# An inverse root moved from ScalarE to guess-and-Newton on GpSimd and VectorE, and one shared-expert product in place of two

## The reference, cut to what matters

```python
shared = dot(silu(dot(h, shared_gate_w.T)) * dot(h, shared_up_w.T), shared_down_w.T)
shared = sigmoid(dot(h, shared_expert_gate_w.T)) * shared
```

```python
normalizer = maximum(abs(C.sum(-1)), exp(-max_log_D))
Cn = C / (normalizer + EPS)
h = einsum('bhst,bhtd->bhsd', Cn, vh)
mu = h.mean(-1); var = ((h - mu) ** 2).mean(-1)
hn = (h - mu) * rsqrt(var + EPS) * ln_scale
x = x + tanh(g_xattn[1]) * hn
```

## Time and profile before

| what | value |
|---|---|
| median of 3 runs | 1719.93 us (1716.78 to 1725.45) |
| the profiled execution | 1727.18 us, of it 1725.9 us span from the first to the last instruction |
| mean granted clock of TensorE | 0.946 of full |
| busy: TensorE, VectorE, ScalarE, GpSimd | 93%, 64%, 59%, 35% of the span |
| expert stage, one full step's vector work | silu 0.60 us, gating 0.69, GpSimd 1.30, cast 0.62, low part 0.69 |
| expert stage ends, cells' loop runs, block begins | about 905, 940 to 1042, 1052 us |

### The profile page before, as it was taken

One profiled execution on the slowest core, in us unless ns is written; L12 is line 12 of the kernel. 1 busy time (PEld: TensorE's weight loads), 2 busy tenths in 40 slices (PEclk: granted clock), 3 DMA queues, 4 the chain that ended last, 5 costly groups with the idle time before them and its releaser, 6 DMA issues.

```text
span 1725.9 us, 30312 instructions
## 1 busy us (share of the span) xinstructions
PE 1598.0 (93%) x10932; PEld 1270.4 (74%) x10932; DVE 1098.8 (64%) x2114; ACT 1016.4 (59%) x2049; POOL 598.6 (35%) x492
## 2 busy tenths in 40 slices
PE   5699999799999999999995994999999999999898
PEld 3256654488888888888882553788888888888687
DVE  5788884487544455444445556776877777776555
ACT  4488888354433344333334663877887887776543
POOL 3333332134345333333330002464464454443000
PEclk8699999799999999999995886999999999999899
DMA  7556663343444333333400003345344334332210
GB/s 219 167 188 205 203 197 113 125 122 105 117 115 114 97 107 107 107 107 108 114 16 9 4 3 110 107 152 172 124 132 131 123 119 151 123 117 68 74 49 25
DMA packets 111046, 196.22 MB, mean 114 GB/s; under 512 B 16721, under 2 KB 59541, under 8 KB 108073
## 3 DMA queue, kind: packets, MB, share of 16 engines
q1 hardware_dynamic: 110898, 194.29, 37.1%
HBM read 167.64 MB, written 25.73 MB: 112 GB/s over the span
## 4 chain that ended last, share of the span: by engine, by line
PE 78%; DVE 8%; ACT 5%; issue 4%; DMA 2%; POOL 1%; SPq 1%; DVEq 0%; POOLq 0%; ACTq 0%
PE bank L67 17%; PE bank L69 17%; PE bank L68 17%; PE bank L282 4%; PE bank L320 4%; PE bank L306 3%; PE bank L1844 3%; PE bank L1812 3%; PE bank L1834 1%; POOL e_hidden L1066 1%; PE bank L1348 1%; PE bank L1347 1%; ACT b_turned L1921 1%; PE bank L1358 1%; PE bank L1367 1%
## 5 line engine op out<-in xcount | busy, mean ns | idle before, releaser
L1066 POOL TENSOR_TENSOR e_hidden<-e_gated,e_comb_wide 128x512 f32<-128x512 f32 x132 | 211.1, 1599 | 347.8 <-DVE e_gated L1031 332.1
L906 ACT CAST e_hidden_hi<-e_hidden 128x512 fp32r<-128x512 f32 x132 | 82.0, 621 | 319.4 <-POOL e_hidden L1066 319.4
L1024 DVE TENSOR_TENSOR e_hidden_lo<-e_hidden,e_hidden_hi 128x512 fp32r<-128x512 f32 x132 | 98.1, 744 | 212.1 <-ACT e_hidden_hi L906 212.1
L69 PE MATMUL bank<-e_x_hi,e_weights_lo 128*128 128x512 f32 (+1 forms) x528 | 210.1, 398 | 0.0
L67 PE MATMUL bank<-e_x_hi,e_weights_hi 128*128 128x512 f32 (+1 forms) x528 | 208.9, 396 | 0.7 <-ACT e_comb_rows L866 0.7
L68 PE MATMUL bank<-e_x_lo,e_weights_hi 128*128 128x512 f32 (+1 forms) x528 | 208.9, 396 | 0.0
L1921 ACT ACTIVATE b_turned<-bank,b_swap_bias 64x512 f32<-64x512 f32 x256 | 175.0, 683 | 32.7 <-PE bank L69 28.3
L527 DVE TENSOR_REDUCE a_negmax<-bank 128x2 f32<-128x512 f32 x256 | 164.7, 683 | 32.3 <-PE bank L282 31.5
L2073 POOL TENSOR_TENSOR b_turned<-b_turned,b_rope_q 128x512 f32<-128x512 f32 x64 | 83.4, 1303 | 237.7 <-ACT b_turned L1921 237.7
L423 ACT ACTIVATE a_exp<-bank 128x512 f32<-128x512 f32 x256 | 143.7, 596 | 18.7 <-PE bank L306 10.0
L69 PE MATMUL bank<-e_weights_hi,e_hidden_lo 128*128 128x256 f32 (+1 forms) x528 | 149.1, 282 | 0.0
(11 more groups left out here) (322 smaller groups left out, 4138.5 us busy)
## 6 DMA issues: line engine op xcount, KB each, us to landing
e_comb_wide<-e_combT SPq DMA_DIRECT2D x130, 256.0 KB, 4.1
e_raw<-in_e_weights SPq DMA_DIRECT2D x64, 384.0 KB, 4.6
b_qk_hi<-b_qk_parts SPq DMA_DIRECT2D x64, 256.0 KB, 2.7
b_qk_lo<-b_qk_parts SPq DMA_DIRECT2D x64, 256.0 KB, 3.0
a_qs<-a_q_parts SPq DMA_DIRECT2D x48, 192.0 KB
a_ks<-a_k_parts SPq DMA_DIRECT2D x48, 192.0 KB
b_qk_parts<-columns SPq DMA_DIRECT2D x32, 256.0 KB, 3.4
b_vw_hi<-b_v_parts SPq DMA_DIRECT2D x16, 512.0 KB, 4.2
```

The source lines that it names most:

```text
L69: return pe.matmul(out, w_lo, x_hi, start=False, stop=stop, skip_group_check=True)
L1024: dve.tensor_tensor(lo[0:rows, :], m.hidden[at % 2][0:rows, :], hi[0:rows, :].bitcast(F32), ALU.subtract).then_inc(s.hidden_lo)
L1066: pool.tensor_tensor(m.hidden[i][0:rows, :], m.gated[i][0:rows, :], m.comb_wide[u % E_RING][0:rows, chunk * BANK:(chunk + 1) * BANK], ALU. ...
```

## The change

**The inverse root.** ScalarE's square root (L1412) goes. VectorE's piece 1 now ends with the sum of squares; the rest of the small work goes to piece 2 (for the last group it stays at piece 1), and ends with a first guess of the inverse root: the bits of the value, read as an integer, times -0.5 plus a constant. Three Newton steps follow, four small instructions each (square, times the value, times -0.5 plus 1.5, times the guess), one more product with the normaliser, and the two wide instructions. This is `finish_cells`. GpSimd runs it for groups 0, 1 and 2, VectorE for group 3. ScalarE waits before a square for `summed` in place of `rooted`, and VectorE at piece 1 of group 2 and 3 for `done` of the group two before.

**The shared expert.** Its gate and up weights lie beside each other, and are used as one operand of 128 columns: one product per step (6 matmuls) gives gate in rows 0 to 63 and up in rows 64 to 127 of one bank. ScalarE reads rows 0 to 63 and writes the silu to rows 64 to 127; everything after that, and the down weights, uses rows 64 to 127. The bank is free for the step after next when `gated` is done, where it was `silu`.

```diff
@@ gate_and_up
-        for which in range(2):
+        for which in range(1 if shared else 2):
             if which == 0 and n >= 2:
-                pe.wait_ge(s.silu, n - 1)
+                pe.wait_ge(s.gated if is_shared(n - 2) else s.silu, n - 1)
...
             for d in range(DK):
-                at = (2 * d + which) * rows
-                last = product(pe, banks[2 * i + which][0:rows, :], [t[:, at:at + rows] for t in m.split[u % E_SPLITS]],
+                at = d * P if shared else (2 * d + which) * P
+                last = product(pe, banks[2 * i + which][:, :], [t[:, at:at + P] for t in m.split[u % E_SPLITS]],
@@ experts_act
-            act.activation(m.silu[i][0:rows, :], banks[2 * i][0:rows, :], ACT.Silu).then_inc(s.silu)
+            gate = slice(0, WIDTH) if is_shared(n) else rows
+            act.activation(m.silu[i][rows, :], banks[2 * i][gate, :], ACT.Silu).then_inc(s.silu)
@@ experts_dve
-            dve.wait_ge(s.up_sums, n + 1)
+            if not is_shared(n):
+                dve.wait_ge(s.up_sums, up_products(n))
...
-            dve.tensor_tensor(m.gated[i][0:rows, :], m.silu[i][0:rows, :], banks[2 * i + 1][0:rows, :], ALU.mult).then_inc(s.gated)
+            up = banks[2 * i] if is_shared(n) else banks[2 * i + 1]
+            dve.tensor_tensor(m.gated[i][rows, :], m.silu[i][rows, :], up[rows, :], ALU.mult).then_inc(s.gated)
@@ cells_act
-        if g >= 0 and piece == 2:
-            act.wait_ge(s.rooted, g + 1)
-            act.activation(m.factor[g % 2][:, :, :], m.factor[g % 2][:, :, :], ACT.Sqrt).then_inc(s.deviation)
...
             if g:
-                act.wait_ge(s.rooted, g)
+                act.wait_ge(s.summed, g)
@@ cells_dve
+            if g >= 2:
+                dve.wait_ge(s.done, g - 1)
...
+            dve.tensor_reduce(factor[:, :, :], m.square[:, :, :, :], AX.X, ALU.add).then_inc(s.summed)
+        if g >= 0 and piece == (2 if g < M_LAST else 1):
+            inv, factor = m.total[g % 2], m.factor[g % 2]
...
+            dve.tensor_scalar(factor[:, :, :], factor[:, :, :], 1.0 / CD, CELL_EPS, ALU.mult, ALU.add).then_inc(own.tick())
             dve.wait_ge(own.sem, own.n)
+            dve.tensor_scalar(m.root[g % 2][:, :, :].bitcast(I32), factor[:, :, :].bitcast(I32), -0.5, ROOT_GUESS, ALU.mult, ALU.add).then_inc(s.rooted)
+    dve.wait_ge(s.rooted, NCHUNK)
+    dve.wait_ge(s.weighed_cells, NCHUNK)
+    finish_cells(k, m, s, dve, own, M_LAST)
...
+def finish_cells(k, m, s, engine, own, g):
+
+    factor, root, step = (t[g % 2][:, :, :] for t in (m.factor, m.root, m.step))
+    for _ in range(ROOT_STEPS):
+        engine.tensor_tensor(step, root, root, ALU.mult).then_inc(own.tick())
+        engine.wait_ge(own.sem, own.n)
+        engine.tensor_tensor(step, step, factor, ALU.mult).then_inc(own.tick())
+        engine.wait_ge(own.sem, own.n)
+        engine.tensor_scalar(step, step, -0.5, 1.5, ALU.mult, ALU.add).then_inc(own.tick())
+        engine.wait_ge(own.sem, own.n)
+        engine.tensor_tensor(root, root, step, ALU.mult).then_inc(own.tick())
+        engine.wait_ge(own.sem, own.n)
+    engine.tensor_tensor(root, root, m.total[g % 2][:, :, :], ALU.mult).then_inc(own.tick())
+    engine.wait_ge(own.sem, own.n)
...
+    engine.tensor_tensor(cells, cells, root.unsqueeze(3).to_broadcast([P, CHUNK, CELLS, CD]), ALU.mult).then_inc(s.scaled)
+    engine.wait_ge(s.scaled, g + 1)
+    engine.tensor_tensor(resid, resid, cells, ALU.add).then_inc(s.done)
@@ cells_pool
+        if g < M_LAST:
+            pool.wait_ge(s.weighed_cells, g + 1)
+            pool.wait_ge(s.rooted, g + 1)
+            finish_cells(k, m, s, pool, own, g)
```

More of the change, by code:

```diff
@@ L630, with is_shared, up_products @@
 TURN = {turn: i + 1 for i, turn in enumerate(TURNS)}
+def is_shared(n):
+    return E_UNITS[E_STEPS[n][0]][1] == PAIRS
 def expert_rows(n):
-    return P if E_UNITS[E_STEPS[n][0]][1] < PAIRS else WIDTH
+    return slice(WIDTH, P) if is_shared(n) else slice(0, P)
+def up_products(n):
+    return sum(not is_shared(v) for v in range(n + 1))
 def route_piece(chunk, n):
@@ L714, in load_comb @@
         for i in range(2 if pair < PAIRS else 1):
[L715 removed]
+            rows = slice(i * WIDTH, (i + 1) * WIDTH) if pair < PAIRS else slice(WIDTH, P)
+            sp.dma_start(m.comb_wide[r][rows, :],
                          io["e_combT"][2 * pair + i:2 * pair + i + 1, cols].broadcast_to([WIDTH, TOKENS])).then_inc(ring["comb_loaded"][r], DMA)
@@ L779, in gate_and_up @@
         u, chunk = E_STEPS[n]
-        (half, _), i, rows = E_UNITS[u], n % 2, expert_rows(n)
+        (half, _), i, shared = E_UNITS[u], n % 2, is_shared(n)
         cols = slice(half * TOKENS + chunk * BANK, half * TOKENS + (chunk + 1) * BANK)
@@ L806, in to_out @@
             tile = chunk * (BANK // P) + t
-            last = product(pe, banks[4 + tile // 2][:, (tile % 2) * D:(tile % 2 + 1) * D], [h[0:rows, t * P:(t + 1) * P] for h in m.hidden_split[n % E_HIDDEN]],
-                           [v[0:rows, GU:] for v in m.split[u % E_SPLITS]], pair == 0 and tile % 2 == 0, pair == PAIRS)
+            last = product(pe, banks[4 + tile // 2][:, (tile % 2) * D:(tile % 2 + 1) * D], [h[rows, t * P:(t + 1) * P] for h in m.hidden_split[n % E_HIDDEN]],
+                           [v[rows, GU:] for v in m.split[u % E_SPLITS]], pair == 0 and tile % 2 == 0, pair == PAIRS)
         last.then_inc(s.out_sums)
@@ L905, in experts_act @@
                 act.wait_ge(s.out_sums, at - E_HIDDEN + 1)
-            act.copy(m.hidden_split[at % E_HIDDEN][0][0:rows, :], m.hidden[at % 2][0:rows, :]).then_inc(s.hidden_hi)
+            act.copy(m.hidden_split[at % E_HIDDEN][0][rows, :], m.hidden[at % 2][rows, :]).then_inc(s.hidden_hi)
         if n < len(E_STEPS):
@@ L1023, in experts_dve @@
             hi, lo = m.hidden_split[at % E_HIDDEN]
-            dve.tensor_tensor(lo[0:rows, :], m.hidden[at % 2][0:rows, :], hi[0:rows, :].bitcast(F32), ALU.subtract).then_inc(s.hidden_lo)
+            dve.tensor_tensor(lo[rows, :], m.hidden[at % 2][rows, :], hi[rows, :].bitcast(F32), ALU.subtract).then_inc(s.hidden_lo)
         if n < len(E_STEPS):
@@ L1091 @@
 M_LATER = 6
+M_LAST = NCHUNK - 1
+ROOT_GUESS = float(0x5f3759df)
+ROOT_STEPS = 3
 def mlstm_memory(k, stack):
     sb = tensors(k, stack, "m")
-    m = namedtuple("m", "ln_scale vaug e_token cell keys log_peak log_gate peak_parts gate_parts e_rows factor total square")
+    m = namedtuple("m", "ln_scale vaug e_token cell keys log_peak log_gate peak_parts gate_parts e_rows factor total root step square")
     return m(sb("ln_scale", [P, D]), sb("vaug", [P, NB, CELLS, CD + 1]), sb("e_token", [P, NB, CELLS]), sb("cell", [P, NB, CELLS, CD + 1]),
@@ L1100, in mlstm_memory @@
              [sb(f"factor{i}", [P, CHUNK, CELLS]) for i in range(2)], [sb(f"total{i}", [P, CHUNK, CELLS]) for i in range(2)],
+             *([sb(f"{n}{i}", [P, CHUNK, CELLS]) for i in range(2)] for n in ("root", "root_step")),
              sb("square", [P, CHUNK, CELLS, CD]))
@@ L1491, in cells_pool @@
 def cells_pool(k, m, w, s):
-    pool = k.nc.gpsimd
+    pool, own = k.nc.gpsimd, k.pool_steps
     pool.wait_ge(s.scale_ready, 1)
```

32 lines of the change are left out of this document (11 added, 21 removed).

## The result

The changed kernel takes 1713.07 us (median of 20 runs, 1708.43 to 1720.91) beside 1721.61 us (20 runs, 1713.09 to 1735.2) for the kernel before on the same chip: ratio 0.994, 95% interval 0.9922 to 0.9957. That is 10.3 us less (7.4 to 13.4), where 11.2 had been predicted. (The ratio is the recorded estimate, and differences in this document are worked out from such ratios; the two medians themselves lie 8.5 us apart.) The time itself, 4.4 us over the forecast of 1708.7, lies in its range. Two more measurements of the same kernel gave 0.9941 (0.9913 to 0.9969) and 0.9955 (0.9931 to 0.9978). The profiled execution took 1716.19 us, its span 1714.8 against 1725.9, with a mean granted clock of 0.951 against 0.946.

What follows compares the result with a forecast made beforehand. The prediction took TensorE, busy 93% of the span, as the bound. Loop 12.56 less tail 5.7 plus shared expert 4.3 gave 11.2 us, so 1719.93 - 11.2 = 1708.7 us, range 1703 to 1715.

Steps and rivals of the forecast that it cites:

- The loop: mLSTM cell loop: without ScalarE's root, its table loads and wait, all batches take 5.15 us; 12.56 us less.
- Rival A: Cell loop: GpSimd's wide instructions hold up VectorE's products, costing 3.6 us; time 1712.3 us, chance 0.1.
- The tail: From the mLSTM's last product to the last addition: 21.0 us against 15.32, so 5.7 us longer.
- the lock: Tail: VectorE and GpSimd get in each other's way; 0.6 us (0 to 2.2) added for GpSimd.
- the lower row of 0.28: Price source for GpSimd's small tail instructions: a cast of 128 elements at 0.28 us, beside a two-input row of 0.42.
- B: Tail: GpSimd's small instructions cost 0.42 us and wide ones 2.7; gain 6.5 us, time 1713.4 us, chance 0.15.
- D: Tail: GpSimd pays a fixed cost per waiting instruction; at 2 us each the kernel is slower, 1730 us, chance 0.03.
- the rule: Tail: VectorE with two SBUF inputs and GpSimd reading SBUF exclude each other for a whole instruction; 1.5 us, not 0.6.
- about 5 us: Sign in the tail: VectorE's gap ahead of its first Newton step, ended by GpSimd's scaling.
- The shared expert: Expert stage: six matmuls in place of twelve per step give 2.8 us in the middle, 1.5 at the end.
- Rival C: Shared expert gives nothing, as a chain of engines sets those steps; gain 6.9 us, time 1713.0 us, chance 0.05.
- The step that failed: Next block's start: its first square root needs a 1.28 us table load, hidden behind VectorE's statistics (2.1 us).

Runs made afterwards that it cites:

- e2: Kernel before with the changed kernel's cell stage (inverse root by guess and Newton steps), shared expert still in two products; 1713.32 us, ratio 0.9909 (4 runs).
- e6: The same kernel as e2, measured a second time: changed cell stage, shared expert as before; 1720.93 us, ratio 0.9964 (12 runs).
- e1: Kernel before with only the changed kernel's experts (shared expert's single product), cell stage as before; 1722.02 us, ratio 0.9972.
- e4: Changed kernel with VectorE's wait for the fourth scaling moved behind group 3's 13 small instructions; 1714.67 us (1 run).
- e8: Changed kernel with one Newton step in place of three, on both engines; 1721.46 us (1 run).
- e11: Changed kernel with VectorE doing groups 2 and 3's small instructions in SBUF, GpSimd group 2's two wide ones behind group 3's scaling; 1712.94 us (1 run).
- e3: Changed kernel with one more square root on ScalarE behind its last squaring, its result read by nobody; 1716.0 us (1 run).

## Why the prediction was right, and where it was not

- **The loop, 12.56 us:** 12.57, and in e2 and e6 the same without the other half. Rival A (GpSimd holds up the loop) falls: no batch from the fourth on takes over 5.15 us in any of the kernels without table loads in the loop. e1 shows that 12.56 was one draw: the same pauses cost 14.3 us at another time.
- **The tail, 5.7 us longer:** 5.37. VectorE's first part 3.35 us (3.27 predicted), GpSimd's 13 small ones 4.94, of which the lock is some 0.1 (4.3 and 0.6), its wide ones 6.4 (7.0), VectorE's last part 5.77 (5.8), two handovers 0.26 (none). GpSimd's small instructions take 0.29 and 0.32 us for products and 0.24 with constants, with 0.08 between; nearest was the lower row of 0.28. So rivals B and D fall: none takes over 0.38 us. The small ones cost 0.5 us more than forecast and the handovers 0.3, the wide ones 0.6 less and the lock 0.5 less. That the sum came within 0.3 us is in part luck.
- **The lock:** it was put at 0.6 us on GpSimd (by the rule 1.5). In the changed kernel the two hardly meet: VectorE has made its guess for group 3 at 1024.60, and GpSimd's first wide instruction begins at 1025.25. So VectorE's gap is 7.06 us, where "about 5 us" was to be the sign. In the kernels in which they do meet (e4, e8, e11), GpSimd's wide instruction began first, or in the same hundredth of a microsecond, and VectorE lost the time.
- **The shared expert, 2.8 + 1.5 us:** 2.69 and 1.52, and alone 2.64 and 1.53 in e1. TensorE's two shared steps start 2.81 apart (2.8 predicted), and the last two gatings 3.36 (3.4). Rival C falls.
- **The step that failed:** "It costs 1.28 us, but VectorE's statistics come first ..., so it is hidden." The load was priced rightly, but taken for something that ScalarE does while it waits. The earlier trace rows made this look safe, for there the load does run ahead of the wait. Here it began when the wait had ended, so all of it was on the path, 1.28 us (e3); why the two places differ is open.
- **The time:** 10.1 us by the touched places, 10.3, 10.2 and 7.8 by the three measurements, 11.2 predicted. Of the 4.4 us by which the median missed 1708.7, some 1.1 are these terms, 1.7 the kernel before, which came out at 1721.61 here and at 1719.93 in the runs that the forecast was set against, and the rest lies in the spread of medians.
